# Graph network on one TensorE-heavy core: the last layer's state turned by DMA and added up by GpSimd instead of turned by TensorE, with VectorE's side work placed anew

## The reference

```python
# block 0: three layers of a gated graph network, one set of GRU weights
h = relu(layernorm(x))
for i in range(3):
    m = h @ weight[i]
    aggr = einsum('bst,bsd->btd', adj != 0, m)
    r = sigmoid(gi_r + gh_r); z = sigmoid(gi_z + gh_z)   # gi = aggr @ w_ih.T + b_ih
    n = tanh(gi_n + r * gh_n)                            # gh = h @ w_hh.T + b_hh
    h = (1 - z) * n + z * h
x = x + h
# block 1: graph attention
h = relu(layernorm(x)); Wh = h @ W.T
e = leaky_relu((Wh @ a1)[:, :, None] + (Wh @ a2)[:, None, :], 0.2)
x = x + softmax(where(adj == 0, -inf, e)) @ Wh
```

## Time and profile before

| | us |
|---|---|
| median of 3 executions | 1818.8 (1817.42 to 1821.85) |
| the profiled execution | 1817.42 |
| its span, first to last instruction | 1815.6 |

### The profile page before, as it was taken

One profiled execution on the slowest core, in us unless ns is written; L12 is line 12 of the kernel. 1 busy time (PEld: TensorE's weight loads), 2 busy tenths in 40 slices (PEclk: granted clock), 3 DMA queues, 4 the chain that ended last, 5 costly groups with the idle time before them and its releaser, 6 DMA issues.

```text
span 1815.6 us, 32208 instructions
## 1 busy us (share of the span) xinstructions
PE 1779.8 (98%) x10500; PEld 945.4 (52%) x10500; DVE 1419.7 (78%) x2827; ACT 1022.8 (56%) x1824; POOL 350.3 (19%) x758
## 2 busy tenths in 40 slices
PE   6999999999999999999999999999999999999995
PEld 5445555545555454555545555454554545555453
DVE  6667878787887878878787887878878777887877
ACT  5556555555556556555565556556555565556553
POOL 1012130311303113031221303113031221303100
PEclk8999999999999999999999999999999999999997
DMA  3322322332314223232322324223232332323121
GB/s 105 76 65 65 70 75 55 85 73 60 96 35 110 52 64 93 66 79 52 87 69 64 81 51 110 52 64 92 51 92 53 78 77 64 75 58 92 32 57 53
DMA packets 323712, 128.38 MB, mean 71 GB/s; under 512 B 239200, under 2 KB 323680, under 8 KB 323680
## 3 DMA queue, kind: packets, MB, share of 16 engines
q1 hardware_dynamic: 323680, 127.97, 29.9%
HBM read 52.96 MB, written 16.78 MB: 38 GB/s over the span
## 4 chain that ended last, share of the span: by engine, by line
PE 96%; issue 1%; DVE 1%; POOLq 0%; POOL 0%; DVEq 0%
PE r_bank L330 27%; PE z_bank L330 27%; PE hn_bank L330 14%; PE in_bank L330 14%; PE s_bank L330 3%; PE w_bank L330 3%; PE nb_bank L345 2%; PE nb_bank L344 2%; PE t_bank L799 1%; PE t_bank L810 1%; DVE dot_terms L1155 0%; DVE x_out L1111 0%; DVE tail_max L1186 0%; PE t_bank L330 0%; DVE u_lo L1201 0%
## 5 line engine op out<-in xcount | busy, mean ns | idle before, releaser
L903 ACT ACTIVATE n_out<-n_pre,bih 128x512 f32<-128x512 f32 x192 | 138.0, 719 | 238.9 <-DVE n_pre L1008 238.6
L330 PE MATMUL hn_bank<-ht_s,wh_hi 128*128 128x512 f16 x768 | 228.4, 379 | 1.7 <-PEq L438 1.7
L912 ACT ACTIVATE ht_s<-ht 128x512 f16<-128x512 f32 x128 | 80.6, 630 | 264.4 <-DVE ht L1024 264.4
L330 PE MATMUL r_bank<-ht_s,wh_hi 128*128 128x512 f16 x768 | 228.5, 379 | 0.0
L330 PE MATMUL z_bank<-ht_s,wh_hi 128*128 128x512 f16 x768 | 228.4, 379 | 0.0
L363 DVE TENSOR_TENSOR nb_lo<-nb_bank,nb_hi 128x512 f16<-128x512 f32 x192 | 131.0, 682 | 84.2 <-ACT nb_hi L359 84.1
L1003 DVE SCALAR_TENSOR_TENSOR n_pre<-tanh_r,hn_b 128x512 f32<-128x512 f32 x192 | 146.3, 762 | 62.2 <-ACT tanh_r L898 57.3
L307 POOL TENSOR_TENSOR ln_gnn<-stats_gnn 128x4 f32<-128x4 f32 x32 | 18.7, 583 | 893.6 <-DVE stats_gnn L260 893.6
L898 ACT ACTIVATE tanh_r<-r_bank,b_rz,down 128x512 f32<-128x512 f32 x192 | 147.2, 767 | 65.8 <-PE r_bank L330 65.7
L893 ACT ACTIVATE hn_b<-hn_bank,b_hn,down 128x512 f32<-128x512 f32 x192 | 147.9, 770 | 57.0 <-PE hn_bank L330 57.0
L907 ACT ACTIVATE tanh_z<-z_bank,b_rz,down 128x512 f32<-128x512 f32 x192 | 146.8, 764 | 26.3 <-PE z_bank L330 26.3
(11 more groups left out here) (248 smaller groups left out, 3938.3 us busy)
## 6 DMA issues: line engine op xcount, KB each, us to landing
x_in<-in_x_dram SPq DMA_DIRECT2D x32, 512.0 KB, 3.9
x_res<-in_x_dram SPq DMA_DIRECT2D x32, 512.0 KB, 4.1
out_dram<-x_out SPq DMA_DIRECT2D x30, 512.0 KB, 5.3
adj_in<-in_adj_dram SPq DMA_DIRECT2D x32, 256.0 KB, 4.0
adj_att<-in_adj_dram SPq DMA_DIRECT2D x32, 256.0 KB, 4.5
h_s<-ht_s SPq DMA_TRANSPOSE x128, 3.0
ht_s<-h_s SPq DMA_TRANSPOSE x64, 3.2
out_dram<-x_out SPq DMA_DIRECT2D x4, 256.0 KB, 2.2
```

The source lines that it names most:

```text
L330: last = nc.tensor.matmul(bank_ap, w, d, start=start and i == 0, stop=stop and i == len(todo) - 1)
L903: nc.scalar.activation(n_out[c][:], n_pre[c][:], ACT.Tanh, bias=bih[:, 4 + c:5 + c]).then_inc(n_ready, 1)
L912: nc.scalar.activation(ht_s[layer % 2][a][:, c, 0, :], ht[a][:, c, :], ACT.Copy, scale=HSCALE).then_inc(ht_hi_ready, 1)
```

## The change

The transposes of the last layer's state leave TensorE in all pairs but the last. In their place `split_last` (ScalarE, VectorE) makes the halves of the last state in `ht_s`, `turn_last` (SyncE) turns them by a DMA transpose into `h_last`, `add_last` (GpSimd) adds the halves into `h_node`, and `residual` (VectorE) adds `h_node` to `x_res`. `whole_state` gets entries of its own in `SIDE`, and waits for the last state's remainder. The mask is a stage `adjacency` of its own. `residual`, `stats_att`, `apply_att`, `split_att`, `dots` and `stats_gnn` get other places. The tail and `LAST_SLOT_SIDE` stay. The core of the diff (declarations, the dictionaries of stages and unchanged lines are left out):

```diff
@@ -57,23 +57,22 @@
...
-    (0, 0): [("residual", 1, 0, -1), ("update", 1, 2, 1, -1)],
-    (0, 1): [("load_gnn", 0, 1)],
+    (0, 0): [("update", 1, 2, 1, -1), ("split_last", 1, 1, -1), ("turn_last", 1, 1, -1), ("add_last", 1, 0, -1)],
+    (0, 1): [("load_gnn", 0, 1), ("apply_att", 0, -1)],
...
-    (0, 3): [("residual", 1, 1, -1), ("split_att", 0, -1)],
-    (0, 4): [("update", 0, 0, 0, 0), ("split_state", 0, 1, 0, 0), ("transpose", 0, 1, 0, 0)],
-    (0, 5): [("neighbours", 1, 0, 1, 0), ("dots", 0, 0, -1)],
-    (0, 6): [("stats_att", 1, -1)],
-    (0, 7): [("dots", 0, 1, -1)],
+    (0, 3): [("add_last", 1, 1, -1), ("split_att", 0, -1)],
+    (0, 4): [("update", 0, 0, 0, 0), ("split_state", 0, 1, 0, 0), ("transpose", 0, 1, 0, 0), ("whole_state", 1, 0, 0), ("whole_state", 1, 1, 0)],
+    (0, 5): [("neighbours", 1, 0, 1, 0)],
+    (0, 6): [("residual", 1, 0, -1), ("residual", 1, 1, -1), ("stats_att", 1, -1)],
+    (0, 7): [("dots", 0, 0, -1)],
...
-    (1, 2): [("neighbours", 0, 1, 0, 0), ("apply_att", 1, -1), ("load_gnn", 1, 1)],
+    (1, 2): [("neighbours", 0, 1, 0, 0), ("dots", 0, 1, -1), ("load_gnn", 1, 1)],
...
-    (1, 5): [("neighbours", 0, 1, 1, 0)],
-    (1, 7): [("split_att", 1, -1)],
+    (1, 5): [("neighbours", 0, 1, 1, 0), ("apply_att", 1, -1)],
...
-    (2, 1): [("softmax", 0, -1), ("dots", 1, 0, -1)],
+    (2, 1): [("softmax", 0, -1), ("split_att", 1, -1)],
...
-    (2, 3): [("dots", 1, 1, -1)],
+    (2, 3): [("dots", 1, 0, -1)],
@@ -86,22 +85,23 @@
...
-    (4, 3): [("stats_gnn", 0, 1)],
-    (4, 4): [("update", 0, 2, 0, 0)],
+    (4, 3): [("adjacency", 0, 1), ("stats_gnn", 1, 1)],
+    (4, 4): [("update", 0, 2, 0, 0), ("split_last", 0, 0, 0), ("turn_last", 0, 0, 0)],
...
-    (4, 7): [("gather", 1, 0, -1)],
-    (5, 0): [("residual", 0, 0, 0), ("update", 0, 2, 1, 0)],
+    (4, 7): [("gather", 1, 0, -1), ("add_last", 0, 0, 0)],
+    (5, 0): [("update", 0, 2, 1, 0), ("split_last", 0, 1, 0), ("turn_last", 0, 1, 0)],
...
-    (5, 2): [("attend", 1, 0, -1), ("neighbours", 0, 0, 0, 1), ("stats_gnn", 1, 1)],
-    (5, 3): [("residual", 0, 1, 0), ("attend", 1, 1, -1), ("load_att", 1, 0), ("store", 1, -1)],
-    (5, 4): [("update", 1, 2, 0, 0)],
-    (5, 5): [("neighbours", 0, 0, 1, 1), ("stats_att", 0, 0)],
-    (5, 6): [("apply_gnn", 1, 1)],
-    (5, 7): [("split_gnn", 1, 1), ("first_transpose", 1, 0, 1), ("first_transpose", 1, 1, 1), ("apply_att", 0, 0)],
+    (5, 2): [("attend", 1, 0, -1), ("neighbours", 0, 0, 0, 1), ("adjacency", 1, 1)],
+    (5, 3): [("add_last", 0, 1, 0), ("attend", 1, 1, -1), ("load_att", 1, 0), ("store", 1, -1)],
+    (5, 4): [("update", 1, 2, 0, 0), ("split_last", 1, 0, 0), ("turn_last", 1, 0, 0), ("whole_state", 0, 0, 1), ("whole_state", 0, 1, 1)],
+    (5, 5): [("neighbours", 0, 0, 1, 1)],
+    (5, 6): [("apply_gnn", 1, 1), ("residual", 0, 0, 0), ("residual", 0, 1, 0), ("stats_att", 0, 0)],
+    (5, 7): [("split_gnn", 1, 1), ("first_transpose", 1, 0, 1), ("first_transpose", 1, 1, 1)],
...
+    (2, 6): [("dots", 1, 1, -1), ("stats_gnn", 0, 1)],
@@ -264,6 +264,8 @@
...
+
+        def adjacency(dve, p, a):
...
@@ -736,6 +743,16 @@
...
+                def turn_last(p, a, c):
+                    if not after_gates(p):
+                        sp.wait_ge(last_lo_ready, per_chunk(p, a, c))
+                        sp.sem_inc(sp_step, 1)
+                        wait_reached(sp, h_node_ready, per_chunk(p, a, c) - 2)
+                        sp.sem_inc(sp_step, 1)
+                        sp.dma_start_transpose(h_last[:, c].rearrange("p s b t -> p (s b) t"),
+                                               ht_s[LAYERS % 2][a][:, c].rearrange("p s t -> p (s t)")).then_inc(
+                                                   h_last_landed[a][c], 16)
+
@@ -788,11 +805,13 @@
...
+                    if not after_gates(p):
+                        return
...
-                    if not (after_gates(p) and a == 1 and c == 1):
-                        wait_reached(pe, x1_ready, per_chunk(p, a, c) - 1)
+                    if not (a == 1 and c == 1):
+                        pe.wait_ge(x1_ready, per_chunk(p, a, c) - 1)
...
-                        wait_reached(pe, sum_ready, per_group(p - 1, 1))
+                        pe.wait_ge(sum_ready, per_group(p - 1, 1))
@@ -907,8 +926,16 @@
...
+                def split_last(p, a, c):
+                    if not after_gates(p):
+                        act.wait_ge(h_ready, per_gate(p, a, LAYERS - 1, c))
+                        nc.scalar.activation(ht_s[LAYERS % 2][a][:, c, 0, :], ht[a][:, c, :],
+                                             ACT.Copy, scale=HSCALE).then_inc(last_hi_ready, 1)
+
...
+                    if layer == LAYERS - 2:
+                        wait_reached(act, h_last_landed[a][c], per_load(p - 1))
@@ -1024,6 +1052,13 @@
...
+                def split_last(p, a, c):
+                    if not after_gates(p):
+                        dve.wait_ge(last_hi_ready, per_chunk(p, a, c))
+                        nc.vector.scalar_tensor_tensor(ht_s[LAYERS % 2][a][:, c, 1, :], ht[a][:, c, :], HSCALE,
+                                                       ht_s[LAYERS % 2][a][:, c, 0, :], ALU.mult,
+                                                       ALU.subtract).then_inc(last_lo_ready, 1)
+
@@ -1040,8 +1075,13 @@
...
-                    dve.wait_ge(res_t_done, per_chunk(p, a, c))
...
+                    if not after_gates(p):
+                        dve.wait_ge(h_node_ready, per_chunk(p, a, c))
+                        nc.vector.scalar_tensor_tensor(part, h_node[c][:], 1.0 / HSCALE, part, ALU.mult,
+                                                       ALU.add).then_inc(x1_ready, 1)
+                        return
+                    dve.wait_ge(res_t_done, 2 * a + c + 1)
@@ -1225,9 +1265,16 @@
...
-                    wait_reached(pool, res_t_done, per_chunk(p - 1, a, c))
+                    wait_reached(pool, last_lo_ready, per_chunk(p - 1, a, c))
...
+
+                def add_last(p, a, c):
+                    if not after_gates(p):
+                        pool.wait_ge(h_last_landed[a][c], per_load(p))
+                        wait_reached(pool, x1_ready, per_chunk(p, a, c) - 2)
+                        nc.gpsimd.tensor_tensor(h_node[c][:], h_last[:, c, 0], h_last[:, c, 1],
+                                                ALU.add).then_inc(h_node_ready, 1)
```

More of the change, by code:

```diff
@@ L592, in _ @@
                     setup_order(fill, {"peaks": reduce_peaks,
-                                       "stats_gnn": lambda p, a: stats_gnn(dve, p, a),
+                                       "stats_gnn": lambda p, a: (stats_gnn(dve, p, a), adjacency(dve, p, a)),
                                        "split_gnn": lambda p, a: split_gnn(dve, p, a),
@@ L620, in graph_blocks @@
         diff = [sb(f"diff{c}", [P, T], F32) for c in range(2)]
+        h_last = sb("h_last", [P, KC, 2, GROUP, P], F16)
+        h_node = [sb(f"h_node{c}", [P, GROUP, P], F32) for c in range(KC)]
         score = sb("score", [P, GROUP, P], F32)
@@ L669, in graph_blocks @@
         res_t_done = sem("res_t_done")
+        h_node_ready = sem("h_node_ready")
+        last_hi_ready, last_lo_ready = sem("last_hi_ready"), sem("last_lo_ready")
+        h_last_landed = [[sem(f"h_last_landed{a}{c}") for c in range(KC)] for a in range(2)]
         gather_done, s2_done, attend_done = sem("gather_done"), sem("s2_done"), sem("attend_done")
@@ L749, in _ @@
                     "tail_store": tail_store,
-                    "probs_transpose": probs_transpose,
+                    "probs_transpose": probs_transpose, "turn_last": turn_last,
                     "transpose": transpose, "first_transpose": lambda *which: first_transpose_sp(sp, *which)})
@@ L989, in _ @@
                     "apply_gnn": lambda p, a: apply_gnn(act, p, a), "apply_att": apply_att, "split_state": split_state,
+                    "split_last": split_last,
                     "neighbours": lambda *which: neighbours_act(act, *which), "split_att": split_att,
@@ L1214, in _ @@
                     "stats_gnn": lambda p, a: stats_gnn(dve, p, a), "split_gnn": lambda p, a: split_gnn(dve, p, a),
-                    "stats_att": stats_att,
-                    "update": update, "split_state": split_state,
+                    "adjacency": lambda p, a: adjacency(dve, p, a), "stats_att": stats_att,
+                    "update": update, "split_state": split_state, "split_last": split_last,
                     "residual": residual, "split_att": split_att, "dots": dots,
@@ L1238, in _ @@
                 all_pairs(pool, lambda *step: None, {
-                    "first_transpose": whole_state,
+                    "whole_state": whole_state, "add_last": add_last,
                     "stats_gnn": lambda p, a: norm_factors(pool, "gnn", p, a, relu_gnn_ready),
```

## The result

The changed kernel takes 1874.99 us (median of 6 executions, 1874.73 to 1876.61), the kernel before 1818.42 (6 executions): a ratio of 1.0312, 95% interval 1.03 to 1.0324. The change costs 56.6 us. The forecast was 1872.

A forecast was written before the change was run, and what follows sets the result against it. Bound: a loop through VectorE, ScalarE and GpSimd, TensorE's work just under it. Stretches 109.2 plus collisions 2.3 and 1.45 make 112.95, 3.6 us a pair more; 15 periods add 54: about 1872 us, range 1800 to 1888.

The forecast's parts named there:

- the loop: Chain through VectorE, ScalarE and GpSimd said to set the period: 109.38 us a pair before, 112.95 after.
- S1: Stretch between updates, (slot 4, step 4) to (5,0): from 13.32 to 11.2 us, ScalarE's wait for GpSimd gone.
- S2: Stretch from the update of (5,0) to that of (5,4): from 9.28 to 7.9 us.
- S5: Stretch from the update of (1,0) to that of (2,0): from 17.22 to 15.7 us.
- S6: Stretch from the update of (2,0) to that of (3,0): from 15.50 to 18.9 us, VectorE waiting for u_hi.
- S7: Stretch from the update of (3,0) to that of (4,4): 27.2 us, unchanged.
- B: Three GpSimd additions in a row at (5,3) and (5,4), holding the update of (5,4): 2.3 us a pair more.
- D: Three GpSimd additions in a row at (0,3) and (0,4), across u_lo and the next update: 1.45 us a pair.
- S3: Stretch from the update of (5,4) to that of (0,4): from 17.38 to 18.9 us without collisions.
- S4: Stretch from the update of (0,4) to that of (1,0): from 9.49 to 9.4 us.
- no collisions: Rival: GpSimd's rows of three additions fall between updates, the loop stays 109.2 us a pair: 1816 us, chance 0.10.
- TensorE sets the pace: Rival: TensorE's own work bounds the kernel, so its cut is time won: 1793, up to 1813 us, chance 0.22.

The follow-up runs named there:

- e1: The kernel before with one of four residual transposes of a chunk left in the loop's pairs, the other three left out: 1817.35 us, ratio 0.9999.
- e10: The kernel before, its transposes still on TensorE, with side work spread much as in the change, nothing left out: 1814.77 us, ratio 0.9983.
- e12: The changed kernel with additions reordered and held, slot 0 and 2 stages moved, group 1's cast u_hi at (2,5) ahead of its remainder: 1795.0 us, ratio 0.9871.
- e2: The changed kernel with GpSimd's additions in the loop's pairs cut to 8 of 512 columns: 1836.26 us, ratio 1.0105.
- e3: The changed kernel with group 1's split_att moved from (2,1), behind the softmax, back to (1,7): 1858.77 us, ratio 1.0231.
- e6: The changed kernel with the same GpSimd additions, whole_state asked for ahead of the last addition instead of behind it: 1849.22 us, ratio 1.0175.
- e11: e10 with one of four residual transposes of a chunk left in the loop's pairs, as in e1: 1796.62 us, ratio 0.988.

## Why the prediction was right, point by point

**The bound.** Right. The kernel before was held by the loop, not by the engine at 98%: e1 shows it directly. TensorE's own work of 109.14 is e10's period. The 107.4 after the change was not reached by any run: e12 has 107.74, and there the loop still seems to be the longer of the two.

**S1, S2, S5, S6, S7.** Right within 0.1 each, for S5 with some luck: its terms as listed add up to 15.9 and not to the 15.7 written. In S1 GpSimd's factors for the other group wait for ScalarE (27.33 us idle at 912.09), which I hadn't seen, so `add_last` of (4,7) falls on `split_gnn` (the addition at 915.08; `split_gnn` at 914.97 takes 2.27 us for two instructions where 935.68 has 1.28). VectorE had to wait for vt_hi there in any case, so 0.15 of the 1.0 comes through (S1 is 11.23, and 11.08 in e2).

**B, the collision of (5,4).** Right in place and kind, mis-sized: the update took 3.98 instead of 2.15, 1.83 and not the forecast 2.3. The additions began at 6.8 us after the update of (5,0), as worked out (6.7). What was mis-sized is how much of the update the additions hold: its first instruction took 0.86, since the addition beside it was near its end, and the other two 1.52 instead of 0.69, 0.17 + 0.83 + 0.83.

**D, the collision of slot 0.** Right in kind, half the size: 0.73 (u_lo 1.96 for 1.23) and not 1.45. The forecast's window for the three additions, 13.9 to 17.4 after the update of (0,0), doesn't fit the trace: they ran from 7.1 to 10.5 after it (943.96 to 947.34, with the update's start at 936.88). Counted from the end of the update of (5,4) at 929.65 it is 14.3 to 17.7, so the forecast seems to name the wrong start, and the times themselves are 0.3 to 0.4 early. S3 was longer than summed (below), so the additions had ended before the update of (0,4) at 948.34 and only u_lo was caught. The price of one instruction held in full, 0.95 by the earlier trace rows, is 0.83 to 0.95 here (B, and the 1.64 of e3); what was wrong each time is how many are held.

**S3 without collisions.** The largest miss: 20.07 (e2), not 18.9. Two steps of it failed. I took the middle between "GpSimd's factors as slow as now" (19.2) and "quick" (18.65), and they were slower than either: ScalarE starts its normalisation 5.88 us after the end of the statistics (941.64 against 935.76), not 5.2. Nearly all of the difference is in the longest of GpSimd's eleven small instructions, 1.57 at 939.76 beside two VectorE instructions with both operands in SBUF, where the kernel before has 1.01 and VectorE idle (timeline of the kernel before, GpSimd):

```profile
991.41 1.01 POOL L322 TENSOR_TENSOR ln_gnn<-ln_gnn,consts 128x4 f32<-128x4 f32 x1
```

The rest is 0.15 of small gaps ahead of it. The sum itself has a hole as well: the terms listed for "quick", with the update before them, add up to 18.0 and not 18.65. One of the two ScalarE instructions that follow the update of (0,0), cast and tanh_r, some 0.6 each, seems to be missing from the list. The collisions were 1.0 too dear and the loop 1.4 too cheap, so the sum missed by only 0.37 a pair: that 1872 came within 3 us of 1875 is in part luck, two errors that met.

**S4.** 9.61 for 9.4; the terms given there make 9.3.

**The queues.** Right. The DMA transposes land in 3.0 us as in the earlier trace rows, and the 60 new ones in 3.1, and TensorE's waits for h_s are 9.1 us in all, 0.6 a pair. GpSimd waits for the landings, as the forecast has it (7.89 us at 924.58, 0.96 at 943.96); they set where its additions start.

**The rival "no collisions"** would have given 1836 and not 1816, by e2; the rival "TensorE sets the pace" comes closest in e12, 1795 where I had 1793. Its condition was the right one (no collisions, the wait for u_hi gone), with one more that I had not named: ScalarE's normalisation in slot 0 must stand behind nb_hi. In e12 one collision of 0.61 is left, and the pace is seemingly still the loop's.

**The Trainium skill's rule** (SBUF — State Buffer, Who interferes with whom), that a tensor_scalar in a two-port mode contends with GpSimd too, agrees with the trace of e6: adj_s, whose only tensor operand is in SBUF, takes 0.61 us beside an addition (912.47 to 913.62) and 0.42 otherwise. Its price here is 0.2 and not the 0.3 I gave, and in the changed kernel nothing, since there adj_s (924.56) began 0.02 before the addition and kept its 0.42.

## What to carry to other kernels

An engine marked busy 98% is not yet the bound: sum the loop through the other engines from one recurring instruction to the next, and if it is as long, shorten it first, or work taken from the busy engine buys nothing. Work handed to GpSimd costs by its place: a row of additions let go by a transfer's landing cost nothing here beside VectorE instructions that read PSUM or wait anyway, and held those with two SBUF operands, up to 0.95 us each (1.64 for 0.69). Where a stage has a half on ScalarE and a half on VectorE, give each half its own place, so that the second doesn't stand waiting for the first.

## What the hardware showed that I had not expected

Contention goes both ways. GpSimd's factor instructions of 128x4 took 0.20 to 0.21 us alone and 0.58 to 0.65 beside VectorE instructions with two SBUF operands, and the long one 1.57 where it took 1.01 in the other group. All eleven took 3.04 us undisturbed (912.09 to 915.13), 5.12 in the kernel before (987.58 to 992.70) and 5.77 on the path of S3 (935.84 to 941.61). A 128x512 addition of two f16 halves took 1.15 us undisturbed, 1.41 and 1.60 beside VectorE.

A removed piece of TensorE work leaves almost no mark in its busy time when the engine isn't the bound: e1 has 0.65 us a pair less busy time for 1.3 us less work at an unchanged period. The waits by instruction show what the busy share hides: VectorE waits for TensorE in e10 and e11, where TensorE is the bound, and not once between 600 and 900 us in any of the other kernels.
